# Moving the expert-row gathers into the second graph layer, and reordering the first stage, of a four-block graph and expert network

## The chip, the cores and the metric

The kernel runs on one core of a Trainium2 chip, as one launch. The metric is device time in microseconds (us) from the launch's start to its end. A core has five engines with queues of their own: TensorE (PE, its weight loads are PEld), VectorE (DVE), ScalarE (ACT), GpSimd (POOL) and SyncE (SP). They meet only through semaphores. [...]

## The reference

There are 6250 nodes with 256 features, 100,000 edges sorted by destination, and a type from 0 to 7 on each edge. Four blocks follow each other, each added to x after a layer norm:

```python
x = x + gnn0(layernorm(x))   # per type r: h = xn @ W[r]; edge scores, softmax per destination, weighted sum of h[src]
x = x + ffn0(layernorm(x))   # argmax of 32 experts: relu(relu(xn @ W1[e] + b1[e]) @ W2[e] + b2[e])
x = x + gnn1(layernorm(x))   # below
x = x + ffn1(layernorm(x))   # top 2 of 8 experts, layer norm, gelu, weighted sum
```

The second graph layer forms one product for every node and then needs, for node i, the rows of edge i alone (the first 6250 edges):

```python
xt = (xn @ weight).reshape(-1, 4, 64)
alpha = softmax(leaky_relu(alpha_l[row] + alpha_r[col], 0.01), axis=1)   # over the 4 heads
tmp = einsum('nh,nhd->nd', alpha[:n], xt[col[:n]])                       # the same for each head
```

## The kernel before, in words

The nodes lie in 49 tiles (NT) of 128 rows (P), the last with 106 rows. `k.x` holds all of x in on-chip memory and stays there through most of the kernel. Every `Stage` has its own buffers and semaphores; its end is a barrier of all engines. Inside a stage each engine has its own program, in the order written, so a wait in it holds all that stands behind it.

**First stage, `relation_rows`.** Loads x, the weights W of the eight types and the attention vectors, and makes for every tile the rows `h_tab` that the edges will gather: `norm.transpose` of the normalised tile, then `product`, eight products of 128 x 264 (L643) and one of 128 x 64 (L648) on PE; ACT copies each to `hb`; SP stores. DVE normalises two tiles ahead (`norm.normalise`, L228) and copies the 64 columns (`half`, L543). Ahead of this loop stand, one after another on DVE: the edge rows (L485), `positions` (L492 to L494), the sums of the first quarter of x (`stats`, L201), the cuts (L504 to L510), the block lines (L513 to L517), the groups (L522 to L533, which end with `at_ok` and let GpSimd gather the edge groups, L365 and L367), the other sums, and the variance and its root for all tiles (`norm.statistics`). Two small products of PE (L628, L630) stand in this chain. On SP the sixteen loads of attention vectors (L411) come after a wait for the first edges (L406), and PE begins only with all of W and all the vectors there (L610). In the tile loop DVE does four pieces of edge work (`turn0` to `turn3`) at tiles 4, 6, 8 and 10 and one (`turn5`) at 30; PE transposes the edge arrays from tile 13 (`TURN0`). GpSimd makes the masks of the windows when `node_tab` has been stored after tile 11.

**`attend0`** sums over the edges of the first layer, with 880 gathers on GpSimd. **`settle`** adds the old x.

**`moe0`** normalises, routes, scatters the rows to their experts, computes them and writes `ys0`. Then (`gather` L1273, `address` L1360, `add` L1366, `tile_stats` L1370) it gathers the result rows of each tile in four buffers, adds them to `k.x` and takes the tile's sums.

**`attend1`** takes mean and root of all tiles (`norm.statistics`), prepares the weights (L1582, L1587, copies L1524 and L1526), and runs the node transform: normalise on DVE, two transposes and the product 128 x 264 on PE (L1598), two copies on ACT (L265 to PE's operand, L1505 to `g`), two stores on SP into `g_tab` and `l_tab` (L1490, L1491). `g` has two buffers, and ACT's copy waits until both stores from the same buffer have landed. When all tables are stored (`tables`), GpSimd gathers two rows a tile (L1471, L1472) in groups of four tiles with two sets of buffers, and DVE does the softmax, the weighted sum and the sums of the new x (L1540 to L1558).

`route1` and `experts1` follow.

## Time and profile before

| | |
|---|---|
| median of 3 runs | 3263.57 us (3260.66 to 3266.58) |
| the profiled execution | 3259.22 us, of which its span is 3257.2 us |
| busy in the span | PE 67%, DVE 55%, ACT 41%, POOL 49% |
| first stage | to about 470 us |
| `attend0`, `settle`, `moe0` up to its last stored row | about 470 to 2006 us |
| gathers and sums of the expert rows | 2006 to 2080 us |
| `attend1` | 2080 to 2320 us |
| `route1` and `experts1` | 2320 us to the end |

The shares are means over stages with different limits. For a change in one stage what matters is which engine or transfer ends each step of that stage. The times of rows are us from the span's start; what stands in brackets is the idle time before an instruction and what ended it.

### The profile page before, as it was taken

The numbers are of one execution on the slowest core, as the hardware profiler recorded it, in microseconds if no ns is written. First come the engines' busy times: TensorE is split into PE (matmuls) and PEld (weight loads), VectorE is DVE, ScalarE is ACT, GpSimd is POOL, SyncE is SP. The second block draws the span as 40 slices with busy tenths as digits, with TensorE's granted clock in tenths as the row PEclk, the third lists the DMA queues.
The fourth block names the chain that finished last, engine by engine and source line by source line (L and its number), as shares of the span: only waits on it lengthen the run. The fifth ranks groups of instructions, "written<-read, shape, count | busy, mean of one in ns | idle before, by whom it ended". The sixth has DMA issues, their size and how long they took to land. (4 is left out here: it accounts for less than half of the span.)

```text
span 3257.2 us, 51141 instructions
## 1 busy us (share of the span) xinstructions
PE 2189.7 (67%) x13091; PEld 1849.9 (57%) x13092; DVE 1780.9 (55%) x4102; ACT 1332.3 (41%) x2969; POOL 1589.4 (49%) x1585
## 2 busy tenths in 40 slices
PE   2999985777777777777626085350430079999998
PEld 1888874656666556565426074230430069999997
DVE  4111125777777777776675434426663365656564
ACT  0444444655565655555301053130111344444443
POOL 1056217777777777777250534327227223334333
PEclk8999986888888888888755588685555589999999
DMA  6355447777765555556542244222302632222221
GB/s 141 126 208 213 193 172 210 214 209 211 208 194 144 145 145 145 144 144 132 53 123 72 78 158 144 68 74 51 97 31 104 210 77 42 46 48 47 48 47 26
DMA packets 225887, 402.34 MB, mean 124 GB/s; under 512 B 58684, under 2 KB 153543, under 8 KB 219086
## 3 DMA queue, kind: packets, MB, share of 16 engines
q0 software_dynamic: 84864, 206.63, 26.2%
q1 hardware_dynamic: 122002, 187.73, 17.3%
q10 hardware_dynamic: 18892, 6.45, 0.9%
q8 instruction: 57, 0.93, 0.1%
q14 instruction: 72, 0.59, 0.1%
HBM read 247.26 MB, written 155.68 MB: 124 GB/s over the span
## 5 line engine op out<-in xcount | busy, mean ns | idle before, releaser
L720 POOL DMA_INDIRECT sum_ring<-h_tab,gnn_edge_row x880 | 839.4, 954 | 268.0 <-issue 260.7
L981 PE MATMUL sum_bank<-sum_ring,sum_one_hot 128*128 128x264 f32 x1760 | 583.0, 494 | 215.2 <-issue 195.7
L981 PEld LDWEIGHTS sum_bank<-sum_ring,sum_one_hot 128*128 128x128 f32 x1760 | 418.7, 247 | 334.5 <-issue 227.0
L1802 POOL DMA_INDIRECT out_dram<-moe_y,moe_to_node x112 | 185.9, 1659 | 383.9 <-ACT moe_y L1828 353.0
L643 PE MATMUL rows_bank<-rows_w_rows,rows_xnT 128*128 128x264 f32 x1568 | 358.6, 387 | 1.7 <-ACT rows_xnT L265 1.7
L643 PEld LDWEIGHTS rows_bank<-rows_w_rows,rows_xnT 128*128 128x128 f32 x1568 | 295.1, 191 | 50.3 <-ACT rows_xnT L265 2.1
L770 ACT ACTIVATE sum_distance_by_lane<-all_iota,gnn_minus_local 128x128 bf16<-128x128 f32 x880 | 267.3, 386 | 0.1
L836 DVE TENSOR_TENSOR sum_ring<-sum_ring,sum_bank 128x1024 f32<-128x1024 f32 x220 | 265.7, 1209 | 0.5 <-ACT sum_ring L784 0.4
L970 PEld LDWEIGHTS sum_bank<-gnn_dst_half,sum_one_hot_T 128*128 128x128 f32 x1760 | 226.2, 205 | 43.9 <-issue 40.3
L970 PE MATMUL sum_bank<-gnn_dst_half,sum_one_hot_T 128*128 x1760 | 230.9, 289 | 28.7 <-ACT sum_one_hot_T L763 14.3
L1960 PE MATMUL moe_bank<-moe_w_low,moe_hidden_high 128*128 x896 | 244.2, 273 | 0.0
L1960 PE MATMUL moe_bank<-moe_w_high,moe_hidden_high 128*128 x896 | 244.2, 273 | 0.0
L1960 PE MATMUL moe_bank<-moe_w_high,moe_hidden_low 128*128 x896 | 244.2, 273 | 0.0
L470 ACT ACTIVATE rows_h_rows<-rows_bank 128x264 f32<-128x264 f32 x392 | 152.9, 390 | 198.5 <-PE rows_bank L643 198.5
L843 DVE TENSOR_TENSOR nodes_acc<-sum_bank,nodes_acc 128x264 f32 x440 | 188.2, 428 | 47.7 <-PE sum_bank L981 19.3
L1844 ACT ACTIVATE moe_hidden<-moe_bank,moe_b_T 128x256 f32<-128x256 f32 x456 | 186.3, 475 | 42.8 <-PE moe_bank L1950 25.5
L543 DVE COPY gnn_dst_half<-rows_bank 128x64 f32<-128x64 f32 x49 | 11.0, 225 | 332.1 <-PE rows_bank L648 332.1
L775 ACT ACTIVATE sum_one_hot<-sum_distance_by_lane,all_ones 128x1024 f32<-128x1024 bf16 x110 | 126.3, 1148 | 147.4 <-PE sum_bank L981 145.5
L1950 PE MATMUL moe_bank<-moe_x_high,moe_w_high 128*128 128x256 f16 x912 | 175.3, 274 | 1.7 <-DVE moe_x_low L1894 1.7
L1950 PE MATMUL moe_bank<-moe_x_low,moe_w_high 128*128 128x256 f16 x912 | 175.3, 274 | 0.0
L1950 PE MATMUL moe_bank<-moe_x_high,moe_w_low 128*128 128x256 f16 x912 | 175.1, 274 | 0.0
L826 DVE TENSOR_TENSOR sum_score<-sum_dst_part,sum_ring 128x64 f32<-128x64 f32 x110 | 24.9, 226 | 266.6 <-DMA sum_ring<-h_tab,gnn_edge_row 266.0
(406 smaller groups left out, 4151.3 us busy)
## 6 DMA issues: line engine op xcount, KB each, us to landing
h_tab<-rows_h_rows SPq DMA_DIRECT2D x49, 1056.0 KB, 3.9
sum_local_rows<-local_tab SPq DMA_DIRECT2D x110, 256.0 KB, 3.8
sorted<-sum_blank_row SPq DMA_DIRECT2D x49, 387.0 KB
moe_stage<-in_L_ffn_W_dram SPq DMA_DIRECT2D x16, 1024.0 KB
moe_tile<-sorted POOLq DMA_DIRECT2D x58, 258.0 KB, 4.1
sum_ring<-h_tab,gnn_edge_row POOLq DMA_INDIRECT x880
sorted<-sum_zero SPq DMA_DIRECT2D x49, 256.0 KB
mask_tab<-rows_masks POOLq DMA_DIRECT2D x7, 1560.0 KB, 7.9
```

Source lines behind the costliest of these rows:

```text
L470: nc.scalar.activation(hb[:, t % 2, r, :], bank[2 + r % 4][:, 0:W0], ACT.Copy).then_inc(h_ok.sem, 1)
L643: last = nc.tensor.matmul(bank[2 + r % 4][:, 0:W0], norm.xT[:, u, c * P:(c + 1) * P], wx[:, c, r, :], start=(c == 0), stop=(c == DC - 1))
L720: nc.gpsimd.indirect_dma_start(ring[:, t % (RING * ST), :], None, k.h_tab, bass.IndirectOffsetOnAxis(k.edge_row[:, t:t + 1], 0)).then_inc( ...
L770: last = nc.scalar.activation(off[:, u * P:(u + 1) * P], k.iota[:, :], ACT.Abs, bias=k.minus_local[:, m * ST + u:m * ST + u + 1])
L836: nc.vector.tensor_tensor(to, to, by, ALU.mult).then_inc(msg_ok, 1)
L843: nc.vector.tensor_tensor(col(k.acc, b), sum_b[g % SG][:, 0:W0], col(k.acc, b), ALU.add).then_inc(added, 1)
L970: last = nc.tensor.matmul(pick_b[n % 2][:, u * R * H0:(u + 1) * R * H0], hotT[:, n % 2, u, :], col(k.dst_half, b[u // G]), start=True, sto ...
L981: last = nc.tensor.matmul(sum_b[j][:, 0:W0], hot[:, m % 2, t, :], ring[:, m % RING * ST + t, :], start=(u == 0), stop=(u == G - 1))
L1802: nc.gpsimd.indirect_dma_start(a["out"], bass.IndirectOffsetOnAxis(to_node[:, n % 2, h:h + 1], 0), y[:, n % 2, h, :], None, bounds_check=N ...
L1844: last = nc.scalar.activation(hg[:, q, m * B1:(m + 1) * B1], bank[q][:, m * B1:(m + 1) * B1], ACT.Gelu, scale=1.0 / (XS * WS), bias=col(b1 ...
L1950: last = nc.tensor.matmul(bank[q][:, m * B1:(m + 1) * B1], w1[pw][:, c, bass.ds(e * F1 + (2 * q + m) * P, P)], xh[px][:, u, c, :], start=( ...
L1960: last = nc.tensor.matmul(bank[6 + u][:, h * D:(h + 1) * D], hh[ph][:, u, m, h * P:(h + 1) * P], w2[pw][:, m, bass.ds(e * D, D)], start=(m ...
```

## The change

Two parts, in two places.

**The expert rows.** `moe0` no longer gathers them; it ends when `ys0` is written. The row numbers are kept as integers in `k.rows0` (one copy of 128 x 49), and the scatters use them directly, without a copy for each tile. `attend1` gathers the rows into eight buffers (`SLOTS`), adds them, takes the sums and makes the node transform in seven chunks of seven tiles (`CH`). On DVE the adds and sums of the next chunk stand between the normalisations of this one; at each chunk's end stand the variance (7 small linked instructions) and, after two adds, the inverse root (5 linked ones), with the square root on ACT between. `g` has eight buffers instead of two, the gathered table rows four sets instead of two, and these gathers take their row numbers from `k.dst_i` and `k.src_i` directly. The sums of the previous group (`tile_stats(n - 1)`) stand in `attend` between the exponents' input and the wait for them. All loops of the stage are written out.

**The first stage.** The attention vectors are loaded first, on SP and ACT side by side; W comes in two halves with a semaphore each; x comes in parts of 6, 12, 15 and 16 tiles, the first on ACT and the others on SP. DVE takes sums, variance and root of the first part alone before the tile loop. All else moves into the loop, at the tiles given in `stats_at` and `turns_at`, and so do the two small products of PE (after tiles 4 and 6). The first edges come in as rows and are turned by PE (two transposes after tile 27).

```diff
-        NF, TURN0 = E // P, 13
+        NF, TURN0 = E // P, 18
...
+        quarter = [0, 6, 18, 33, NT]
...
+            def load_x(j):
+                t0, t1 = quarter[j], min(quarter[j + 1], NT - 1)
+                sp.dma_start(k.x[:, t0:t1, :], a["x"][t0 * P:t1 * P, :].rearrange("(t p) f -> p t f", p=P)).then_inc(loaded[j], 16)
+            vectors(sp, 0, "L0_gnn_attn_src")
+            for j in range(2):
+                sp.dma_start(wn[:, j * R // 2:(j + 1) * R // 2], a["L0_gnn_W"][j * R // 2:(j + 1) * R // 2].rearrange("r (c p) f -> p r c f", p=P)).then_inc(weights[j], 16)
...
+                load_x(1)
                 sp.dma_start(k.first_s.rearrange("(t o) -> t o", o=1), a["dst"][0:NF * P].rearrange("(t p) -> t p", p=P)[:, 0:1]).then_inc(first_st, 16)
...
                     sp.dma_start(rows(k.h_tab.rearrange("(n r) o -> n (r o)", r=R), t * P, P), flat(hb[:, t % 2, :, :])).then_inc(stored.sems[t % 2], 16)
-                    if t == 11:
+                    if t == 1:
+                        sp.wait_ge(rows_ok, 1)
+                        sp.dma_start(k.row_s[0:E].rearrange("(p e) -> p e", p=EP), e_row[:, :]).then_inc(line_st, 16)
+                    if t == 8:
+                        sp.wait_ge(at_ok, 1)
+                        sp.dma_start(k.block_tab.rearrange("(c p) -> p c", p=P), blk[:, :]).then_inc(block_st, 16)
+                    if t == 10:
+                        sp.wait_ge(block_st, 16)
+                        sp.dma_start(blk_row[:, :], line(k.block_tab)).then_inc(block_in, 16)
+                    if t == 4:
+                        sp.wait_ge(pos_ok, 1)
+                        for j, name in enumerate(("dst", "src")):
+                            sp.dma_start(ends_n[:, j, :], a[name][0:NPAD].rearrange("(t p) -> t p", p=P)).then_inc(first_nodes, 16)
...
 
         @block.scalar
...
+            vectors(act, 1, "L0_gnn_attn_dst")
+            act.dma_start(k.x[:, 0:quarter[1], :], a["x"][0:quarter[1] * P, :].rearrange("(t p) f -> p t f", p=P)).then_inc(loaded[0], 16)
...
+            root(0)
+            norm.t_ok.start(act)
...
+                if t in (3, 10, 16):
+                    root((3, 10, 16).index(t) + 1)
...
+            turns_at = {1: edge_rows, 2: positions, 3: cuts, 5: block_lines, 7: groups, 9: turn0, 11: turn1, 13: turn2, 15: turn3, 26: first_edges, 28: keep_first, 32: turn5}
+            stats_at = {0: (stats, 1), 1: (variance, 1), 3: (scales, 1), 6: (stats, 2), 8: (variance, 2), 10: (scales, 2),
+                        12: (stats, 3), 14: (variance, 3), 16: (scales, 3)}
...
+                if t in stats_at:
+                    stage, j = stats_at[t]
+                    stage(j)
...
+                if t == 4:
+                    pe.wait_ge(need_ok, 1)
+                    nc.tensor.matmul(bank[7][0:NT, 0:1], k.before[0:NT, 0:NT], need[:, :], start=True, stop=True).then_inc(start_ps, 1)
+                if t == 6:
+                    pe.wait_ge(diag_ok, 1)
+                    nc.tensor.matmul(bank[7][:, 8:8 + 3 * NT], k.ones[0:NT, :], diag[:, :, :].rearrange("p j b -> p (j b)"), start=True, stop=True).then_inc(lines_ps, 1)
+                if t == 27:
+                    pe.wait_ge(first_ok, 1)
+                    pe.wait_ge(turn_free, 3 * G)
+                    for j in range(2):
+                        last = nc.tensor.transpose(bank[7][:, j * P:j * P + NT], ends_nf[:, j, :], k.ident[0:NT, 0:NT])
+                    last.then_inc(first_ps, 1)
                 if TURN0 <= t < TURN0 + 3 * G:
                     n, j = divmod(t - TURN0, G)
```

```diff
-                pool.sem_inc(begun, 1)
-                nc.gpsimd.indirect_dma_start(k.xs0, bass.IndirectOffsetOnAxis(ids[0:m, u:u + 1], 0), xi[0:m, u, :], None).then_inc(scattered[u], 16)
-            rounds(pool, NT, 4, scatter)
...
-                t = i * 4 + u
-                m = P if not isinstance(t, int) or t < NT - 1 else TAIL
-                pool.wait_ge(row_ok, NT + t + 1)
-                pool.sem_inc(begun, 1)
-                nc.gpsimd.indirect_dma_start(y[0:m, u, :], None, k.ys0, bass.IndirectOffsetOnAxis(ids[0:m, u:u + 1], 0)).then_inc(gathered[u], 16)
-            rounds(pool, NT, 4, gather)
 
         @block.sync
...
-        g = s.sb("rows_out", [P, 2, W])
-        ids = s.sb("rows", [P, 2, 2, 4], I32)
-        got, left = s.sb("gathered", [P, 2, 4, W]), s.sb("row_half", [P, 2, 4, H1])
+        g = s.sb("rows_out", [P, SLOTS, W])
+        got, left = s.sb("gathered", [P, SETS, 4, W]), s.sb("row_half", [P, SETS, 4, H1])
...
+            for t in range(NT):
+                m = P if t < NT - 1 else TAIL
+                if t >= SLOTS:
+                    pool.wait_ge(node_ok, t - SLOTS + 1)
+                nc.gpsimd.indirect_dma_start(y[0:m, t % SLOTS, :], None, k.ys0, bass.IndirectOffsetOnAxis(k.rows0[0:m, t:t + 1], 0)).then_inc(brought[t % SLOTS], 16)
             pool.wait_ge(tables, 1)
...
+            for n in range(GROUPS + 1):
+                if n >= SETS:
+                    pool.wait_ge(used, n - SETS + 1)
+                for u in range(size(n)):
+                    t = n * 4 + u
+                    nc.gpsimd.indirect_dma_start(got[:, n % SETS, u, :], None, k.g_tab, bass.IndirectOffsetOnAxis(k.dst_i[:, t:t + 1], 0)).then_inc(arrived[n % SETS], 16)
+                    nc.gpsimd.indirect_dma_start(left[:, n % SETS, u, :], None, k.l_tab, bass.IndirectOffsetOnAxis(k.src_i[:, t:t + 1], 0)).then_inc(arrived[n % SETS], 16)
...
+            for t in range(NT):
+                sp.wait_ge(g_ok, t + 1)
+                sp.dma_start(k.g_tab[t * P:(t + 1) * P, :], g[:, t % SLOTS, :]).then_inc(stored[t % SLOTS], 16)
+                sp.dma_start(k.l_tab[t * P:(t + 1) * P, :], g[:, t % SLOTS, D + H1:W]).then_inc(stored[t % SLOTS], 16)
...
+            for c in range(CHUNKS):
+                root(c)
+                keep(c * CH)
+                for t in range(c * CH, (c + 1) * CH):
+                    if t + 1 < (c + 1) * CH:
+                        keep(t + 1)
+                    emit(t)
```

The main loop of DVE in `attend1`, and its end:

```diff
+            for c in range(CHUNKS):
+                more = c + 1 < CHUNKS
+                t0, t1 = c * CH, (c + 1) * CH
+                if more:
+                    add(t1)
+                    add(t1 + 1)
+                scales(c)
+                for j in range(CH):
+                    normalise(t0 + j)
+                    if more:
+                        if j + 2 < CH:
+                            add(t1 + j + 2)
+                        stats(t1 + j)
+                if more:
+                    variance(c + 1)
...
+            for n in range(GROUPS + 1):
+                attend(n)
+            tile_stats(GROUPS)
```

## Rows read from the trace of the kernel before

**Rows 1.** Page, costliest groups: the edge gathers on GpSimd.

```profile
L720 POOL DMA_INDIRECT sum_ring<-h_tab,gnn_edge_row x880 | 839.4, 954 | 268.0 <-issue 260.7
```

**Rows 2.** Timeline of the first 83 us: start us, us, engine, line, operation.

```profile
23.71 4.12 SPq L411 DMA_DIRECT2D rows_attn_blocks<-in_L_gnn_attn_src_dram  x8
...
39.30 6.07 PE L616 MATMUL rows_bank<-all_ident,rows_w_natural 128*128 128x128 f32 x32 [39.30 <-DMA rows_attn_blocks<-in_L_gnn_attn_dst_dram]
...
45.21 8.36 PE L623 MATMUL rows_bank<-rows_attn_blocks,rows_w_natural 128*128 128x16 f32 x64
...
54.20 1.28 ACT L222 ACT_TABLE_LOAD   x1
...
79.01 0.74 DVE L228 TENSOR_SCALAR rows_xn<-nodes_acc,rows_mean,rows_rstd 128x256 f32<-128x256 f32 x2 [0.25 <-DVE rows_rstd L286]
...
82.30 8.79 PE L643 MATMUL rows_bank<-rows_w_rows,rows_xnT 128*128 128x264 f32 x32 [1.70 <-ACT rows_xnT L265]
```

**Rows 3.** DMA issues of 0 to 90 us: count, KB each, median us to landing.

```profile
rows_w_natural<-in_L_gnn_W_dram SPq DMA_DIRECT2D x1, 2048.0 KB, 19.3
...
rows_group_rows<-row_line,rows_edge_of_group POOLq DMA_INDIRECT x4, 8.5
```

**Rows 4.** Timeline, two neighbouring tiles late in the first stage.

```profile
442.43 0.23 DVE L543 COPY gnn_dst_half<-rows_bank 128x64 f32<-128x64 f32 x1 [7.19 <-PE rows_bank L648]
...
450.17 0.22 DVE L543 COPY gnn_dst_half<-rows_bank 128x64 f32<-128x64 f32 x1 [7.19 <-PE rows_bank L648]
```

**Rows 5.** Timeline of the first stage: edge tables on VectorE, gathers and masks on GpSimd.

```profile
56.39 0.31 DVE L522 COPY rows_block_lines<-rows_bank 128x147 f32<-128x147 f32 x1
...
61.97 0.99 POOL L365 DMA_INDIRECT rows_group_rows<-row_line,rows_edge_of_group  x1 [16.70 <-DVEq L534]
...
122.61 1.13 DVE L548 TENSOR_SCALAR rows_valid<-rows_lane,rows_of_group 128x256 f32<-128x256 f32 x4
...
353.30 0.84 POOL L391 DMA_DIRECT2D mask_tab<-rows_masks  x1 [0.30 <-POOL rows_masks L389]
```

**Rows 6.** Timeline from the first expert-row gather to the second graph layer.

```profile
2006.54 1.02 POOL L1273 DMA_INDIRECT moe_y<-results,moe_rows  x1 [10.65 <-SPq L1293]
...
2009.56 0.42 DVE L1366 TENSOR_TENSOR nodes_acc<-nodes_acc,moe_y 128x256 f32 x1 [6.67 <-DMA moe_y<-results,moe_rows]
...
2013.63 1.40 DVE L1370 BATCH_NORM_STATS2 nodes_stats<-nodes_acc  x4
...
2077.33 0.43 DVE L1370 BATCH_NORM_STATS2 nodes_stats<-nodes_acc 128x6 f32<-128x256 f32 x1
...
2080.05 0.24 DVE L271 TENSOR_TENSOR gnn_tmp<-nodes_stats 128x49 f32<-128x49 f32 x1 [2.29 <-PEq L116]
```

**Rows 7.** Timeline of the node transform, its start and end.

```profile
2088.35 0.69 DVE L1524 COPY gnn_wT<-gnn_bank 128x512 f32<-128x512 f32 x1 [4.76 <-PE gnn_bank L1582]
...
2093.20 2.12 PE L1598 MATMUL gnn_bank<-gnn_w,gnn_xnT 128*128 128x264 f32 x4
...
2096.69 1.06 PE L1598 MATMUL gnn_bank<-gnn_w,gnn_xnT 128*128 128x264 f32 x4
...
2097.80 1.06 PE L1598 MATMUL gnn_bank<-gnn_w,gnn_xnT 128*128 128x264 f32 x4
...
2171.85 0.39 ACT L1505 ACTIVATE gnn_rows_out<-gnn_bank 128x264 f32<-128x264 f32 x1 [1.25 <-DMA l_tab<-gnn_rows_out]
...
2175.99 0.98 POOL L1471 DMA_INDIRECT gnn_gathered<-g_tab,gnn_rows  x1 [95.87 <-issue]
```

**Rows 8.** Waits of 2092 to 2172 us: total us, times, longest.

```profile
ACT gnn_rows_out L1505 <- DMA l_tab<-gnn_rows_out: 38.8, 44, 1.7
```

**Rows 9.** Windows at its end: busy of PE, PEld, DVE, ACT, POOL; PEclk, DMA share, GB/s.

```profile
2172.00:2174.00 2.00, 0.00 (x0) 0.00 (x0) 0.00 (x0) 1.52 (x2) 0.00 (x0) 1.00 0.30 75
2174.00:2176.00 2.00, 0.00 (x0) 0.00 (x0) 0.00 (x0) 0.00 (x0) 0.01 (x1) 0.53 0.00 0
```

**Rows 10.** Groups by line on GpSimd, 2176 to 2310 us.

```profile
L1471 POOL DMA_INDIRECT gnn_gathered<-g_tab,gnn_rows x49 | 55.6, 1134 | 110.5 <-issue 110.5
```

More of the change, by code:

```diff
@@ L344, in relation_rows, with vectors @@
         block = s.block()
+        def vectors(eng, j, name):
+            eng.wait_ge(cleared, 1)
+            with nc.allow_non_contiguous_dma(reason="attention vectors, one word a lane"):
+                for h in range(H0):
+                    p0 = h * HD0 % P
+                    eng.dma_start(ablk[p0:p0 + HD0, h * HD0 // P, j * H0 + h:j * H0 + h + 1],
+                                  a[name][h:h + 1, :].rearrange("a b -> b a")).then_inc(attn_in, 16)
         @block.gpsimd
@@ L456, in _, with root @@
                 nc.scalar.activation(wd[:, c, :].rearrange("p (r h) -> p r h", r=R), got_v[:, c, :, 1, :], ACT.Copy).then_inc(v_ok, 1)
-            norm.root(act)
+            def root(j):
+                part = slice(quarter[j], quarter[j + 1])
+                act.wait_ge(norm.var_ok, j + 1)
+                nc.scalar.activation(norm.sd[:, part], norm.var[:, part], ACT.Sqrt).then_inc(norm.sd_ok, 1)
+            root(0)
+            norm.t_ok.start(act)
             h_ok.start(act)
-            with nc.allow_non_contiguous_dma(reason="the first edges, one word a node"):
-                for t, name in ((k.dst_i, "dst"), (k.src_i, "src")):
-                    act.dma_start(t[:, :], a[name][0:NPAD].rearrange("(t p) -> p t", p=P)).then_inc(first_nodes, 16)
             norm.keep(act, 0, 0, d_ps)
             for t in range(NT):
+                if t in (3, 10, 16):
+                    root((3, 10, 16).index(t) + 1)
                 if t + 1 < NT:
@@ L533, in _, with variance @@
-            ch.link(nc.vector.tensor_copy(at_i[:, :], got[:, 1, :]))
-            v.sem_inc(at_ok, 1)
-            for j in range(1, 4):
-                stats(j)
-            norm.statistics(v, ch)
+                for t in range(quarter[j], quarter[j + 1]):
+                    last = nc.vector.bn_stats(k.stats[:, t, :], k.x[:, t, :])
+                ch.link(last)
+            def variance(j):
+                part = slice(quarter[j], quarter[j + 1])
+                moments(nc, ch, *(k.stats[:, part, i] for i in (1, 2, 4, 5)), norm.mean[:, part], norm.var[:, part], norm.tmp[:, part])
+                v.sem_inc(norm.var_ok, 1)
@@ L539, in _ @@
+            norm.xn_ok.start(v)
             d_ok.start(v)
@@ L1497, in _ @@
         def _(act):
-            norm.root(act)
-            g_ok.start(act)
-            def emit(i, u):
-                xt_ps.done(act, i * 2 + u)
-                stored.slot(act, i, u)
-                nc.scalar.activation(g[:, u, :], bank[2 + u][:, 0:W], ACT.Copy).then_inc(g_ok.sem, 1)
-            norm.keep(act, 0, 0, xt_ps)
-            with act.Fori(0, (NT - 1) // 2) as i:
-                for u in range(2):
-                    norm.keep(act, i * 2 + u + 1, 1 - u, xt_ps)
-                    emit(i, u)
@@ new lines, in add, with stats, variance @@
+            def add(t):
+                v.wait_ge(brought[t % SLOTS], 16 * (t // SLOTS + 1))
+                m = P if t < NT - 1 else TAIL
+                nc.vector.tensor_tensor(k.x[0:m, t, :], k.x[0:m, t, :], y[0:m, t % SLOTS, :], ALU.add).then_inc(node_ok, 1)
+            def stats(t):
+                v.wait_ge(node_ok, t + 1)
+                nc.vector.bn_stats(k.stats[:, t, :], k.x[:, t, :]).then_inc(stat_ok, 1)
+            def variance(c):
+                part = slice(c * CH, (c + 1) * CH)
+                v.wait_ge(stat_ok, (c + 1) * CH)
+                moments(nc, ch, *(k.stats[:, part, i] for i in (1, 2, 4, 5)), mean[:, part], var[:, part], tmp[:, part])
+                v.sem_inc(var_ok, 1)
@@ new lines, in scales, with normalise @@
+            def scales(c):
+                part = slice(c * CH, (c + 1) * CH)
+                v.wait_ge(sd_ok, c + 1)
+                rsqrt_newton(nc, ch, rstd[:, part], tmp[:, part], var[:, part], sd[:, part])
+            def normalise(t):
+                if t >= 2:
+                    v.wait_ge(t_ps, t - 1)
+                nc.vector.tensor_scalar(xn[:, t % 2, :], k.x[:, t, :], mean[:, t:t + 1], rstd[:, t:t + 1], ALU.subtract, ALU.mult).then_inc(xn_ok, 1)
+            add(0)
+            for t in range(1, CH):
+                add(t)
+                stats(t - 1)
@@ L1523, in _ @@
+            stats(CH - 1)
+            variance(0)
             v.wait_ge(wt_ps, 1)
```

328 lines of the change are left out of this document (149 added, 179 removed).

## Prediction

> **What bounds the kernel now.** I read the page first: no engine is busy over 67% of the span, so stages have to be read one by one. In the sum over edges GpSimd issues 880 gathers, and busy plus idle give (839.4 + 268.0) / 880 = 1.26 us for each [rows 1]. That is GpSimd's pitch; the stage runs at it, whatever PE does, and the change leaves it alone. Then I read the timeline where the change acts.
>
> In the first stage PE does nothing until 39.30 us, prepares weights until about 53.6, and starts the first tile's product only at 82.30 [rows 2]. DVE is the one that is late: its serial chain of edge work, all sums, and root ends with the first normalisation at 79.01, and ACT's issue of two slow DMAs stands in the 3.29 us after it. From there a tile takes 450.17 - 442.43 = 7.74 us, and DVE waits 7.19 of them for PE [rows 4]. So the loop is bound by PE, and its 49 tiles slide as a whole with their start. In it DVE has over 7 us free in each tile.
>
> From 2006.54 to 2077.33 + 0.43 the expert rows come in, one in each 1.26 us; DVE waits for them, and PE is idle [rows 6]. Only then come the root and the node transform: first product at 2093.20, first gather from its tables at 2175.99 [rows 7]. In it PE could take a tile in 2097.80 - 2096.69 = 1.11 us, but ACT waits 38.8 us for stores from its two buffers [rows 8], so a tile takes about 1.6 us ((2171.85 - 2093.20) / 49). The last part, 98 gathers, belongs to GpSimd again.
>
> **The first stage, part by part.** What has to be there before the first product is now: W, x of six tiles, the vectors. The vectors need 8 issues on each of two queues, at 4.12 / 8 = 0.52 us each [rows 2], so W is issued near 5.5 us. W of 2 MB took 19.3 us to land, behind 6 MB of x [rows 3]; now about 2.8 MB have to come before or with it. I bound its landing by 16 and 25 us after the start (the full 19.3 after 5.5 is the upper bound) and take 19, nearer to the lower end, since most of x has moved behind it. The first half is turned meanwhile, so half of 6.07 us remains: 22. The 64 thin products take 8.36 us: 30.5. ACT's copies and root and five small instructions on DVE make 1.8 (an estimate, some 0.2 each [rows 6]), the table load 1.28, and from normalisation to product 1.7 (3.29 in the rows, less ACT's DMA issues): 35.3 [rows 2]. The granted clock might fall during the thin products, which would add up to 3 us; I take 36.5. Gain: 82.30 - 36.5 = 45.8, between 40 and 50.
>
> What moved into the loop must fit. DVE runs two tiles ahead, so an insert may last about 7 us (a tile less one normalisation) before PE waits. The sums of x take 16 x 0.35 = 5.6 us at most (0.35 from four in 1.40 us [rows 6]); the longest arithmetic piece, the groups, took 61.97 - 56.39 = 5.6 us plus 0.7 for four small ones [rows 5]. Both fit, just. Waits are the danger. `turn0` at tile 9 waits for gathers that depend on `groups` at tile 7. By the sum above, `half(7)` is at 36.5 + 9.4 + 7 x 7.74 = 100.1 (9.4: the first tile, 8.79 and the thin product); `groups` ends at 106.3; eight gathers at 1.26 and 8.5 us of landing [rows 1, 3] end at 124.9; with its own 1.8 us (four of 1.13 in all, and a copy [rows 5]) and a normalisation, DVE is ready at 127.1. PE wants that tile at the end of product 10, 123.1. So PE stands about 4 us; with stores of the loop beside these gathers I take 5, between 0 and 15, since nothing shows these gathers under that load. Cuts (tile 3) wait for row numbers that are stored two tiles earlier, which fits by about a tile. Two small products and two transposes on PE cost 1.2 us together. SP's new waits at tiles 1, 4, 8 and 10 stand behind a store with nothing urgent after them; node numbers leave SP after tile 16 instead of 11, but at nearly the same time (16 x 7.74 + 36.5 against 11 x 7.74 + 82.3), so GpSimd's masks still end near 353, far from the stage's end [rows 5]. If that cover went, the stage would end with the masks.
>
> Sum of the first part: 45.8 - 5 - 1.2 = 39.6, range 24 to 50.
>
> **The expert rows and the node transform.** The scatters lose a DVE copy per tile but run at GpSimd's 1.26: nothing. The stage now ends with the last stored result, near 2006.2; a barrier took 2080.05 - 2077.76 = 2.3 us, so the new stage starts near T = 2008.5 and its last sum of 2077.8 no longer counts [rows 6]. From T:
> - First sum after 0.3 + 3.0 (2009.56 - 2006.54), six more at 1.26, an add, a sum: T + 11.7 [rows 1, 6].
> - Variance, seven small linked instructions. The same on 49 columns takes 0.24 each [rows 6]; for 7 columns I take 0.19: T + 13.0. The copies of the weights took until 2.8 us after 2088.35 [rows 7]: T + 15.9. Two adds and five small ones: T + 17.6.
> - A full chunk: DVE needs 1.08 us a tile (an add, a sum, a normalisation, 0.35 to 0.37 each in a run), PE 1.11 [rows 7]: 7.8. At the seam stand the last sum 0.35, variance 1.3, two adds 0.75, scales 0.95; with hand-overs 3.4. So 11.2 us, six times, is 67.2. GpSimd needs 7 x 1.26 = 8.8 for the same tiles and has eight buffers, so it stays ahead.
> - The last chunk 7.8, then turn, product and copy 2.6: T + 95.2. From ACT's last copy (2171.85 + 0.39) to the first gather took 3.75 [rows 7]: T + 99 = 2107.5, against 2175.99. The eight store buffers end the waits of 38.8 us [rows 8], but SP still needs two issues per tile, about 1.05 us at the pitch of rows 2, just under PE's pitch.
>
> Gain 68.5. Bounds: if DVE's instructions don't overlap at all (1.24 us a tile, links at 0.24) a chunk is about 13 and the gain 55; if the gathers set the pace (48 x 1.26 + 3.3, then a last chunk and tail of 17) it is 86.
>
> The 98 table gathers never waited for their two sets: idle before them is issue [rows 10]. Four sets and row numbers without a copy therefore give nothing. Their mean of 1134 ns against 954 comes in stretches where DVE works on long operands, and that stays [rows 1, 10]. In the final group four sums of 1.40 us now stand before the wait for the exponents instead of in idle time: 1.1 us lost. Second part: 67.4, range 50 to 85.
>
> **Sum.** 3259.22 - 39.6 - 67.4 = 3152.2. The median of the runs lies 4.35 above the profiled execution: 3156.
>
> **A rule of the Trainium skill against this.** After the node transform, with PE idle, the granted clock is still 1.00 (2.4 GHz) from 2172 to 2174, and 0.53 on average in the next two microseconds, so it falls to 0.50 (1.2 GHz) [rows 9]. At the low level four products took 2.12 us, at the high 1.06 [rows 7]. The Trainium skill, "TensorE: Matmul & The Clock Gate", "HAM oscillation — how this bites in real kernels", says that pauses between bursts of matmuls can bring the clock down again each time. Here each seam of chunks makes such a pause; by that rule the time would be that of the first rival.
>
> **The rivals.**
> - *The clock falls at every seam.* For it: rows 9, and a pause of PE that I estimate at 2 to 2.5 us (the seam less PE's last tile). Against: in those rows it is still up in the first stretch after PE's last work. Price: two tiles per chunk at 2.7 instead of 1.11, about 3 us, less a little caught up, times seven: 19. Time 3175. Chance 0.15.
> - *Waits in the first loop hold PE again and again.* For it: five inserts wait for a DMA or PE, and W took 19.3 us to land once [rows 3]. Against: most have a tile or more of slack. Four more stalls of a tile: 31 us; time 3187. Chance 0.15.
> - *The gathers, not DVE, set the chunks' pace* (if adds and sums overlap better and seams are cheaper): 3156 - 17 = 3139. Chance 0.1.
> - *The new stage doesn't overlap:* sums first, then the transform, because gathers run late under a busy DVE. Only the first part and the store waits remain, about 60: 3204. Chance 0.03.
> - *Slower:* PE runs the first loop at the low clock, as it would if DVE's inserts broke up its work. Eight times 2.12 instead of 1.06 is 8.5 us a tile; from 13 of the 49 tiles on (107 / 8.5) the change loses, at 20 tiles the time is 3156 + 170 = 3326. Against: before, the loop ran beside masks and four turns without one pause. Chance 0.02.
>
> **How the numbers follow.** The forecast has 0.55, range 3138 to 3174. The range for 8 in 10 takes in the first and third rival and most of the second: 3130 to 3190. About 0.2% (6.5 us) is what a measurement of this kernel can tell from no change; slower by more has 0.02, within it 0.01, faster 0.97.
>
> **What would show it.** First stage: the first L643-like product near 36 us; the first loop's end near 425 instead of 465; PE's only pause near 123 us, before the transpose of tile 12; a later start of W would show in PE's first row. Second: the stage begins near 2008 less the first gain; chunks of 11 us on DVE, with PE idle at their seams alone; ACT's waits for stores gone; granted clock 1.00 through the chunks; the first table gather 99 us after the stage's start; 133 us for the gathers as before. The prediction would be wrong if a chunk took over 14 us, if PE paused in several tiles of the first loop, or if the table gathers changed their pitch.

## The result, and the profile after

The changed kernel takes 3162.49 us (median of 4 runs, 3159.72 to 3165.93), where the kernel before takes 3265.07 (3260.66 to 3267.99): ratio 0.9685, with a 95% interval of 0.967 to 0.970. Forecast were 3156, with 3138 to 3174 as its range and 3130 to 3190 as the range for 8 in 10. The profiled execution took 3159.72 us, 7.5 more than the sum of 3152.2.

The gain is 99.1 us of span (3257.2 to 3158.1). The seams of the stages divide it (a load here is a group of four tiles, taken at its first issue; all in us):

| stretch | forecast | measured |
|---|---|---|
| start to the first scatter to the experts (1809.95, now 1773.98) | -39.6 | -36.0 |
| scatters of the rows to the experts' order (68.5, now 68.3) | 0 | -0.3 |
| first to last load of the experts' tiles (114.9, now 122.7) | 0 | +7.9 |
| last load to the first table gather (182.65, now 115.35) | -68.5 | -67.3 |
| from there to the end (1081.2, now 1077.8) | +1.1 | -3.4 |

The timeline of the first 50 us after, against [rows 2] (in all rows a name with q, as SPq, is the queue or sequencer of that engine):

```profile
12.85 5.13 PE L675 MATMUL rows_bank<-all_ident,rows_w_natural 128*128 128x128 f32 x32 [12.85 <-DMA rows_w_natural<-in_L_gnn_W_dram]
...
17.82 9.39 PE L683 MATMUL rows_bank<-rows_attn_blocks,rows_w_natural 128*128 128x16 f32 x64
...
26.80 8.05 SPq L412 DMA_DIRECT2D nodes_acc<-in_x_dram  x2
...
32.25 5.75 PE L699 MATMUL rows_bank<-rows_w_rows,rows_xnT 128*128 128x264 f32 x16
34.89 4.14 SPq L430 DMA_DIRECT2D nodes_acc<-in_x_dram  x1
39.08 2.49 SPq L432 DMA_DIRECT2D node_tab<-rows_row_zero  x1
41.65 1.24 ACT L495 ACTIVATE rows_h_rows<-rows_bank 128x264 f32<-128x264 f32 x4 [9.03 <-SPq L90]
42.10 5.51 PE L699 MATMUL rows_bank<-rows_w_rows,rows_xnT 128*128 128x264 f32 x16 [4.10 <-ACT rows_h_rows L495]
```

W's first half is there at 12.85, and PE turns both halves without a pause, where all of W was forecast for 19; so the first product starts at 32.25 instead of 36.5. But it stops after four of its eight relations: ACT waits 9.03 us for SP's line 90. That line opens the row buffers (`stored.start(sp)`), and in SP's order it stands behind the issues of x and one small store, which take from 26.80 to 41.57; before them SP stood 6.1 us until the first edges had landed (L426). The first tile ends at 48.04, 15.8 us after its start instead of the 9.4 of the forecast.

The same loop at tiles 8 to 11, against [rows 4, 5]. The four rows of L596 (`half`, L543 before) mark the ends of tiles 8, 9, 10 and 11; the last line is the only wait of PE from 117 to 132 (total us, times, longest):

```profile
110.86 0.22 DVE L596 COPY gnn_dst_half<-rows_bank 128x64 f32<-128x64 f32 x1 [1.03 <-PE rows_bank L704]
...
118.60 0.23 DVE L596 COPY gnn_dst_half<-rows_bank 128x64 f32<-128x64 f32 x1 [5.55 <-PE rows_bank L704]
118.62 3.73 PE L699 MATMUL rows_bank<-rows_w_rows,rows_xnT 128*128 128x264 f32 x16
...
124.53 1.24 ACT L495 ACTIVATE rows_h_rows<-rows_bank 128x264 f32<-128x264 f32 x4 [5.33 <-DMA h_tab<-rows_h_rows]
124.97 5.47 PE L699 MATMUL rows_bank<-rows_w_rows,rows_xnT 128*128 128x264 f32 x16 [2.62 <-ACT rows_h_rows L495]
...
128.71 1.14 DVE L601 TENSOR_SCALAR rows_valid<-rows_lane,rows_of_group 128x256 f32<-128x256 f32 x4 [9.89 <-DMA rows_group_dst<-dst_line,rows_edge_of_group]
...
130.87 0.23 DVE L596 COPY gnn_dst_half<-rows_bank 128x64 f32<-128x64 f32 x1
...
138.95 0.22 DVE L596 COPY gnn_dst_half<-rows_bank 128x64 f32<-128x64 f32 x1 [6.41 <-PE rows_bank L704]
```

```profile
PE rows_bank L699 <- ACT rows_h_rows L495: 2.6, 1, 2.6
```

Three tiles take 138.95 - 110.86 = 28.1 us, where three times 7.74 are 23.2: a stall of the length that was forecast, 4.9 us. PE waits 2.62 of them, and then four relations take 5.47 us instead of 3.73, at a lower clock (0.84 on average from 118 to 129). Two waits stand there: DVE's for the edge groups, as forecast, and ACT's for a stored row, which was not. And the one that holds PE in this kernel is ACT's, in the middle of tile 10's product. By the time PE comes to the transposes of tile 12, DVE's wait is just over (128.71, normalised at 130.9). Had ACT not held it, PE would have come there near 126.1 and waited 4.8 us for DVE (an estimate: one tile earlier 7.5 us lie between the product's start at 110.88 and the next transposes at 118.40).

A seam of chunks in the second graph layer, where [rows 7] had one loop (the last row is the first gather from the tables):

```profile
2005.42 0.17 DVE L274 TENSOR_TENSOR gnn_tmp<-gnn_tmp 128x7 f32<-128x7 f32 x1
...
2007.98 0.39 ACT L1541 ACTIVATE gnn_rows_out<-gnn_bank 128x264 f32<-128x264 f32 x1 [0.50 <-PE gnn_bank L1666]
2008.27 0.20 ACT L1529 ACTIVATE gnn_sd<-gnn_var 128x7 f32<-128x7 f32 x1
...
2008.50 0.20 DVE L282 RECIPROCAL gnn_rstd<-gnn_sd 128x7 f32<-128x7 f32 x1 [1.39 <-ACT gnn_sd L1529]
...
2010.06 0.44 PE L1658 MATMUL gnn_bank<-all_ident,gnn_xn 128*128 128x128 f32 x2 [2.11 <-DVE gnn_xn L1580]
...
2080.32 0.98 POOL L1503 DMA_INDIRECT gnn_gathered<-g_tab,nodes_dst_i  x1 [29.64 <-SPq L1522]
```

The variance is there at 2006.2, but ACT takes the root only behind its last two copies (DVE waits 1.39 us for it), and PE stands 2.11 us. The reciprocals, one for each chunk, start at 1995.62, 2008.50, 2019.38, 2032.14, 2042.97, 2055.47 and 2066.31: three chunks of 10.8 to 10.9 us, and three of 12.5 to 12.9. The windows say why (busy time of PE, PEld, DVE, ACT and POOL, then the granted clock, DMA share, GB/s):

```profile
1996.00:2002.00 6.00, 4.45 (x13) 3.36 (x14) 5.53 (x19) 1.54 (x4) 4.60 (x5) 0.50 0.35 106
2002.00:2023.00 21.00, 15.47 (x79) 12.03 (x79) 16.40 (x60) 9.28 (x28) 13.79 (x15) 0.99 0.85 176
2023.00:2027.00 4.00, 4.00 (x15) 3.08 (x14) 3.19 (x11) 1.44 (x4) 3.12 (x3) 0.61 0.57 150
2027.00:2047.00 20.00, 14.78 (x76) 11.58 (x75) 16.06 (x60) 8.73 (x27) 11.61 (x12) 0.99 0.82 163
2047.00:2050.00 3.00, 3.00 (x10) 2.36 (x9) 2.54 (x9) 1.43 (x4) 2.39 (x3) 0.50 0.62 132
2050.00:2073.00 23.00, 18.15 (x93) 14.29 (x93) 14.94 (x55) 10.54 (x32) 0.68 (x1) 1.00 0.37 101
```

The clock is low in three of seven chunks, the long ones: the first from its start, behind a long idle stretch, and the other two only after PE has resumed work behind a seam. At 2021.15 PE's transposes still take 0.44 us and at 2022.13 too, and only the four products from 2022.41 on take 1.65 and then 1.97 us instead of 1.06. The pause before these two chunks was 2.33 and 2.06 us, those before the chunks of 10.8 to 10.9 us 2.07 to 2.11.

### The profile page after: what moved, and what is told of

Read it like the earlier page. It is cut to its first block and busy times, and to the rows that moved or that the text cites. A ratio compares the mean times of both kernels' runs of the same rounds, so it can differ in the third digit from the quotient of the medians.

```text
span 3158.1 us, 49641 instructions
## 1 busy us (share of the span) xinstructions
PE 2201.9 (70%) x13093; PEld 1863.9 (59%) x13094; DVE 1782.5 (56%) x4090; ACT 1326.0 (42%) x2973; POOL 1590.8 (50%) x1585
## 5 line engine op out<-in xcount | busy, mean ns | idle before, releaser
L596 DVE COPY gnn_dst_half<-rows_bank 128x64 f32<-128x64 f32 x49 | 11.0, 225 | 295.6 <-PE rows_bank L704 295.6
```

## The experiments

Two halves first. Both are the changed kernel with functions of the kernel before put back: in the first `moe0` and `attend1`, in the second `relation_rows`.

**The first stage alone.**

> The new first stage alone; the expert rows are gathered and the second graph layer runs as in the kernel before. If the two parts of the change are independent, the first loop's barrier comes 37 us earlier, as in the changed kernel's trace (433.3 instead of 470.6), and all behind it shifts by as much: 3265 - 37 = about 3228 us median. Rival: the middle of the program pays for an earlier start. In the changed kernel the loop over the experts' tiles ran 7.9 us longer (124.8 instead of 116.9) with the granted clock at 0.50 for longer; if the first stage's new timing does that, the loop is 124 to 125 us here too and the median is about 3236. If the 7.9 us belong to the changed second half, the loop is 117 here.

Measured: 3236.06 us (3227.99 to 3242.58), ratio 0.990 (0.987 to 0.993). The first scatter comes at 1775.34, 34.6 us earlier than before (36.0 in the whole), so the stage gives nearly what it gives in the whole. The loop over the experts' tiles took 130.8 us, though this half leaves its code as it was: the rival's 3236 is met, but by a longer loop than its 124 to 125. Which of the moves within the stage gives how much was not run.

**The second half alone.**

> The first stage as before; gathers of the expert rows, sums, statistics and node transform in chunks of seven, eight row buffers. If independent: the stretch from the end of the experts' tiles to the first gather of the tables shrinks by about 65.5 us (168.5 from the seam at 2009.6 to the old first table gather less the 102.0 from the new stage's start), so 3265 - 65 = about 3200 us median, or 3208 if the loop over the experts' tiles is longer here (125 us instead of 117). Rival: the two parts help each other; then this and the first stage alone together fall short of 102 us or go over it by more than 8.

Measured: 3199.15 us (3191.76 to 3205.16), ratio 0.980 (0.977 to 0.983). From the stage's first gather to the first table gather it takes 100.8 us; before 169.5, in the changed kernel 101.2. The experts' loop took 114.6 us. The halves add up to 29.4 + 66.3 = 95.7 us of medians against 102.6 for the whole; the 7 us between are less than the 16 by which the experts' loop differs from profile to profile. That loop's clock, for the kernel before, the changed kernel and the first stage alone, from the loop's first load on:

```profile
1878.00:1890.00 12.00, 8.73 (x37) 7.07 (x37) 0.90 (x4) 3.52 (x11) 5.63 (x11) 0.50 0.31 96
1890.00:1902.00 12.00, 10.94 (x73) 9.40 (x74) 4.97 (x16) 6.99 (x26) 4.02 (x8) 0.97 0.52 168
```

```profile
1842.00:1854.00 12.00, 9.17 (x37) 7.31 (x38) 0.90 (x4) 3.77 (x12) 5.87 (x11) 0.50 0.33 99
1854.00:1866.00 12.00, 12.00 (x42) 9.98 (x42) 3.23 (x10) 4.39 (x14) 2.82 (x6) 0.50 0.40 121
1866.00:1878.00 12.00, 11.63 (x64) 10.15 (x63) 4.45 (x15) 5.36 (x17) 2.15 (x4) 0.73 0.38 120
```

```profile
1844.00:1856.00 12.00, 9.43 (x38) 7.62 (x39) 0.90 (x4) 3.80 (x12) 5.99 (x12) 0.50 0.36 103
1856.00:1868.00 12.00, 10.94 (x75) 9.37 (x74) 4.96 (x16) 6.84 (x24) 3.96 (x8) 0.99 0.53 169
1868.00:1880.00 12.00, 12.00 (x49) 10.00 (x49) 4.34 (x13) 5.52 (x16) 2.89 (x6) 0.58 0.48 153
1880.00:1892.00 12.00, 12.00 (x47) 10.45 (x48) 3.12 (x11) 3.94 (x12) 2.16 (x4) 0.50 0.31 101
```

Once the first loads are through, PE at the low level is busy all the time with 42 to 49 instructions in 12 us, instead of 73 to 75. The clock comes up once and stays (before), comes up late (changed), or comes up, falls under a busy PE and comes up again (first stage alone).

**The row buffers opened early.** In `relation_rows`:

```diff
+            stored.start(sp)
             vectors(sp, 0, "L0_gnn_attn_src")
...
                 sp.dma_start(k.node_tab[0:1, :], ends_f[:, :]).then_inc(node_st, 16)
-                stored.start(sp)
```

> The changed kernel, with the two increments that open the row buffers put ahead of everything else that SP issues. Theory: ACT's fifth copy waited for them, since SP reaches them only after it has issued the loads of x (26.8 to 41.6), and PE stood behind ACT; the first tile took 15.8 us instead of 9.2. Without that wait the first half row is kept near 41.4 instead of 48.0 and the barrier comes 6.6 us earlier: about 3156 us median. Rival: PE waits for something else next (a half of W, x, or tile 9's gathers, whose own chain starts from the loads and not from the loop): then tile 0 is faster but PE stands longer before tile 12 (4.9 us in the changed kernel, up to 11.5 here), and the median stays at 3162.

Measured: 3157.53 us (3150.58 to 3168.57), ratio 0.967 (0.965 to 0.970). The medians' difference from 3162 is within the scatter; the profile isolates the effect:

```profile
31.96 8.56 PE L699 MATMUL rows_bank<-rows_w_rows,rows_xnT 128*128 128x264 f32 x32
...
40.95 0.23 DVE L596 COPY gnn_dst_half<-rows_bank 128x64 f32<-128x64 f32 x1 [9.01 <-PE rows_bank L704]
```

All eight relations run in one piece, the first tile ends 7.1 us earlier, and so does the last (421.00 instead of 428.12). At the first scatter to the experts 3.3 of the 7.1 us are left (1770.73 instead of 1773.98); from the loop's end to there the profiles on chips with fast transfers differ by up to 5 us anyway. The stall at tiles 9 to 11 stays at 4.9 us: the gathers start from the loop's tile 7 and slide with it.

**The turning two tiles later.** In `relation_rows`; the store of the node rows and the reload of their ends move by two tiles as well:

```diff
-7: groups, 9: turn0, 11: turn1, 13: turn2, 15: turn3,
+7: groups, 11: turn0, 13: turn1, 15: turn2, 17: turn3,
-        NF, TURN0 = E // P, 18
+        NF, TURN0 = E // P, 20
```

> The changed kernel, with the four steps that turn the gathered edge groups moved from tiles 9, 11, 13, 15 to 11, 13, 15, 17 and what hangs on them two tiles later. Theory: DVE stood 9.9 us at tile 9 for the gathers of the edge groups, and PE 4.9 us behind it; tile 11 starts DVE's part at about 134, by when the gathers have landed (128.7), so both waits go and the barrier comes 4.9 us earlier: about 3158 us median. Cost: the masks end some 15 us later, near 361, still under the loop that ends at 428. Rival: a later chain (masks or gates) then ends last, and nothing is gained or some us are lost.

Measured: 3164.07 us (3159.80 to 3167.24), ratio 0.968 (0.966 to 0.971). DVE's wait is gone, the stall is not: 112.14 to 140.15 for the same three tiles, 28.0 us.

```profile
119.90 12.86 SPq L436 DMA_DIRECT2D h_tab<-rows_h_rows  x2
...
126.34 1.24 ACT L495 ACTIVATE rows_h_rows<-rows_bank 128x264 f32<-128x264 f32 x4 [5.86 <-DMA h_tab<-rows_h_rows]
126.78 5.20 PE L699 MATMUL rows_bank<-rows_w_rows,rows_xnT 128*128 128x264 f32 x16 [3.16 <-ACT rows_h_rows L495]
```

The store of tile 8 lands late while the edge groups' gathers run, ACT has no free buffer for tile 10, and PE waits 3.16 us for ACT. So my reading of the stall by DVE's wait alone fell. Two kernels separate the two waits:

**Three row buffers, alone and with the later turning.** `hb` gets a third slot and the stores a third semaphore; `turned` lies over `wn`.

```diff
-        stored = Landed(s, "h_rows_stored", 2)
+        stored = Landed(s, "h_rows_stored", 3)
-        hb = s.sb("h_rows", [P, 2, R, W0])
+        hb = s.sb("h_rows", [P, 3, R, W0])
```

> The changed kernel with three buffers of stored rows in the first stage instead of two (the third takes the place of the turned edge groups, which are laid over the weights' natural copy, no longer read by then). The changed kernel's tile 10 ends 12.3 us after tile 9 instead of 7.7: ACT waited 5.3 us there for a store that landed late while the edge groups' gathers ran. At the same place DVE waited 9.9 us for those gathers. Moving DVE's part away alone gave nothing: tile 10 still took 12.5 us. Theory now: each of the two waits alone holds PE by about 4.5 us, so the third buffer alone gives nothing either: tiles 9 to 11 take 20.3 us (15.5 without a stall). Rival: only the late store matters, and DVE's wait is covered: tiles 9 to 11 take 15.5 to 16 us and the first loop ends 4.5 us earlier.

> Both at once: three buffers of stored rows, and the turning of the edge groups two tiles later. Theory: with both waits gone tiles 9 to 11 take 15.5 us and the first loop ends 4.5 to 5 us earlier than in the changed kernel (its last half row at 423.5 for a first one at 48.0). Rival: the gathers slow something else, and some of the 4.5 us stays.

Both ran, once each, on a chip with slower transfers (the kernel before takes 3605 us there), so they are compared with each other within the first loop. The two expectations count from the end of tile 9 to that of tile 11, two tiles (20.3 us, or 15.5 without a stall); here, as above, three are counted, from the end of tile 8. The third buffer alone takes 110.06 to 140.28, 30.2 us; both together 112.50 to 135.72, 23.2 us, which is three tiles without any stall. With the third buffer alone PE no longer waits for ACT, but 4.91 us for DVE:

```profile
128.16 1.14 DVE L601 TENSOR_SCALAR rows_valid<-rows_lane,rows_of_group 128x256 f32<-128x256 f32 x4 [9.19 <-DMA rows_group_dst<-dst_line,rows_edge_of_group]
...
130.41 0.69 PE L236 MATMUL rows_bank<-all_ident,rows_xn 128*128 128x128 f32 x2 [4.91 <-DVE rows_xn L228]
```

Two waits in parallel, and each by itself costs the three tiles 4.8 us or more (4.8 for ACT's, 7.0 for DVE's on the chip with slower transfers): taking away either gives nothing. Of the 4.9 us that go with both, the loop as a whole keeps less. From the first half row to the last it takes 377.0 us where the changed kernel takes 380.1, because with the later turning tiles 33 and 34 take 9.12 and 8.13 us instead of 7.74 each.

**No seams.** In `attend1`: the last sums and the variance of the next chunk move ahead of this chunk's last normalisation, and ACT's root ahead of its copies; PE and ACT lead by a tile across chunks.

```diff
-                        stats(t1 + j)
-                if more:
-                    variance(c + 1)
+                        if j + 2 < CH:
+                            stats(t1 + j)
+                        elif j + 2 == CH:
+                            stats(t1 + j)
+                            stats(t1 + j + 1)
+                            variance(c + 1)
...
+            for t in range(NT):
+                if t % CH == CH - 2 and t + 2 < NT:
+                    root(t // CH + 1)
```

> The changed kernel with the seams between the chunks of seven closed: the next chunk's last statistics and its variance go ahead of the last normalisation but one, ACT takes the root before its last copies instead of behind them, and PE and ACT lead by a tile over the seam. Theory: a chunk takes 7.8 us of work and some 3.4 us of seam, in which PE stands 2.1 to 2.5 us for ACT's root (2008.27) that comes 2.1 us after the variance (2006.2). Without seams the loop of 49 tiles takes about 49 x 1.11 = 54.4 us plus its cold start, so the first gather of the tables comes near T+83 to T+88 instead of T+102: 14 to 19 us less, 3146 us median give or take the experts' loop. The granted clock, which fell to 0.50 at two of the seams, should then stay at 1.0 after the first chunk. Rival: the gathers (1.25 us each) become the pace: 49 of them and 7 before the loop give 61.3 us and the table gathers start no earlier than T+88.

Measured: 3156.23 us (3154.05 to 3161.98), ratio 0.966 (0.964 to 0.969). First gather to first table gather: 90.4 us, 10.8 less than the changed kernel's 101.2, where 14 to 19 were expected. Only 6.3 of them show in the medians; in the profiled execution the experts' loop took 129.9 us instead of 122.7. The clock stays up, but a chunk takes 9.9 us and not 7.8:

```profile
2011.00:2063.00 52.00, 44.37 (x228) 34.46 (x227) 48.27 (x171) 26.46 (x80) 32.78 (x31) 0.99 0.85 180
```

DVE is busy 48.27 of 52 us. With the seam closed its twelve small instructions per chunk (some 2.3 us) no longer stand in a gap, and 7 x 1.08 + 2.3 = 9.9. DVE is the bound there, neither PE (44.37) nor the gathers (32.78).

**One chunk of 49** (`CH = 49`): sums first, then the loop.

> The changed kernel with one chunk of 49 tiles: all sums and statistics first, then one root and the whole loop; the order within the stage is that of the kernel before, in the new stage. This is the change without its overlap. Theory: sums at the pace of the gathers, 3.8 + 48 x 1.25 = T+64, variance, root and scales 2.5, then the loop without seams 49 x 1.11 + 4 = 58: the first gather of the tables at T+126 to T+130, 24 to 28 us later than in the changed kernel, so 3187 us median. Rival: the overlap is worth more, as the forecast's fourth case had it (3204, 45 us more), or nothing, if the seams cost as much as the overlap gives (3162).

Measured: 3201.53 us (3194.66 to 3204.96), ratio 0.979 (0.977 to 0.982), 39 us above the changed kernel. From first gather to first table gather 135.9 us, 34.7 more than in the changed kernel, between the theory's 24 to 28 and the rival's 45. That the median comes out near the rival's 3204 is not all the stage's doing: in the profiled execution (3204.96) the experts' loop took 131.1 us, 8.3 more than in the changed kernel's.

**Two store buffers** instead of eight for `g`.

> The changed kernel with two buffers instead of eight for the rows that are stored to the tables (the sums keep their eight). Theory: a buffer comes free only when its store has landed, some 2.9 to 3.4 us after the copy, so two tiles take that long and the pace is 1.7 us a tile, as in the kernel before (49 tiles in 83 us), instead of 1.11: 49 x 0.6 = 29 us more less what the seams hide (2 us each), so the first gather of the tables at T+115 to T+131 and about 3180 us median. Rival: with the sums between the tiles the stores are hidden: no change, 3162.

Measured: 3200.56 us (3191.74 to 3220.34), ratio 0.981 (0.977 to 0.986); 143.5 us, more than either theory had. The waits of the stage:

```profile
ACT gnn_rows_out L1542 <- DMA l_tab<-gnn_rows_out: 46.7, 27, 4.8
...
DVE gnn_rstd L282 <- ACT gnn_sd L1530: 42.4, 6, 8.5
```

Beside the gathers a store is waited for up to 4.8 us, where the longest wait in [rows 8] was 1.7. And the root of the next chunk stands in ACT's queue behind two copies that wait so: 42.4 us of DVE's time at six seams, where the changed kernel has 8.4. That step was in neither theory, and its 34 us are most of the 42.3 by which the stretch grew. Together with the last experiment: neither overlap nor buffers 169.5 us (the kernel before, which has a barrier in this stretch as well), overlap with two buffers 143.5, eight buffers without overlap 135.9, both 101.2.

**Two sets** of table rows (`SETS = 2`).

> The changed kernel with two sets of four table rows in flight instead of four. Theory: POOL issues the 98 gathers back to back, 1.13 to 1.33 us each, and never waits for DVE in either kernel, so the sets are worth nothing: first to last table gather 130 us as before, 3162 us median. Rival: with two sets POOL waits for DVE (attention of four tiles takes some 10 us): the stretch grows by 2 us or more.

Measured: 3163.97 us (3155.64 to 3169.52), ratio 0.968 (0.966 to 0.971). First to last table gather 130.5 us against 130.1: the sets give nothing.

**Everything at once:** early opening, three row buffers, later turning, no seams.

> All that the runs speak for: the row buffers opened before SP's loads (-7.1 us in the first tile), three row buffers and the turning two tiles later (-4.5), and no seams in the node transform (-14 to -19). Sum: 26 to 31 us under the changed kernel's 3162, about 3133 us median; the experts' loop adds or takes up to 10 by its granted clock. Rival: the gains of the first stage are lost again in the sum over the edges behind it, and only the seams count: 3146.

> The kernel with everything at once, again: on the chip of its first run the kernel before took 3605 us, and every kernel's transfers were slower in the sum over the edges (156 GB/s there instead of 217 in the same stretch), so that run stands beside the others by its ratio alone (0.9659, as much below 1 as the changed kernel's 0.9685). Measured one by one the parts give 7.1 (row buffers opened early), 3 to 5 (third buffer with the later turning) and 10.8 (no seams): where the kernel before takes 3265, about 3141 us median, ratio 0.962. Rival: the 21 us are lost for the most part in the stretches between (a longer low clock in the experts' loop): 3155 or more, ratio 0.966 again.

Measured: 3482.89 us and ratio 0.966 (0.963 to 0.969) on the chip with slow transfers; on the second one 3145.82 us (3138.51 to 3158.95), ratio 0.963 (0.961 to 0.966). Its last half row is copied at 418.79 instead of 428.12, tiles 9 to 11 take 23.2 us, and the seam stretch 89.5. It is the fastest here, some 17 us under the changed kernel. The two stretches give the 21 us that were expected (9.3 and 11.7), and the experts' loop, at 127.1 us, takes 4.3 of them back in the profiled execution.

## Why the prediction was right

The forecast of 3156 stands 6.5 us from 3162.49, but its misses have both signs. Of the span's gain 3.6 us too many were forecast up to the first scatter, 7.6 in a middle that was taken as unchanged and 1.2 up to the first table gather, and 4.5 too few from there to the end. Both gains are there with the causes that were named, except where a line below says otherwise.

- *First product at 36.5:* 32.25. The term for W was too large: the thin products ended at 27.2 instead of 30.5. The rest of the sum held (5.0 us from there to the product, 4.8 forecast), and the thin products took 9.39 instead of 8.36, at a granted clock of 0.75 against 0.85 before: the fall that I had allowed for.
- *The first tile takes 9.4:* 15.8. This step missed a queue: `stored.start(sp)` stands behind SP's issues of x, which were moved past it. I had followed what SP's new waits hold up and not what an increment behind its long issues releases. The first two misses cancel for the most part (-4.3 and +6.4), which is luck, and the early opening shows the second by itself.
- *PE stands 5 us before tile 12:* 4.9 us, but inside tile 10's product, and what held PE in the changed kernel was ACT's wait for a late store (2.62 us, and 1.74 more at the lower clock). DVE's wait, the named cause, is real, and it would have been sufficient, as three row buffers alone show; here it was hidden behind the other. The size came out right because two waits of like length end at one place. That is luck too.
- *Masks hidden:* the last of them go out at 345.33, far ahead of 428. *Elsewhere PE doesn't pause:* from the first product to 430 PE waits for ACT at these two places only (4.1 and 2.6 us). The other tiles take 7.74 us, nine of them 8.1 to 8.3 with small products or transposes of PE in them. So the rival of repeated waits fell. The granted clock is 1.00 on average from 50 to 428, so the slower case fell too.
- *The middle unchanged:* it was 7.6 us longer, the largest miss of the sum. The experts' loop is 114.6 to 131.1 us long in the profiled executions of this study (114.6 for three changed kernels and 114.9 before, 130.8 and more for two others), with the granted clock at 0.50 for longer in the long ones. The half that leaves this loop's code alone had 130.8 and the half that changes `moe0` 114.6, so a long loop does not need the edit to `moe0`. That the new timing of the first stage makes a long loop likelier is not excluded: the two profiled kernels with the old first stage had 114.9 and 114.6, those with the new one 114.6 to 131.1, and the first stage alone gave 29.4 us of median where its first scatter came 34.6 us earlier. What sets the length stays open. It fits the scatter of some 10 to 20 us between runs of one kernel (the kernel before ran in 3259.55 us at a mean clock of 0.804 and in 3278.97 at 0.794), but that this loop makes that scatter was not shown.
- *Chunks of 11.2:* 10.8 to 10.9 at the high clock, 12.5 to 12.9 where it fell. PE's pause at the seam was 2.11 us (2 to 2.5 forecast), 1.39 of it passed on from DVE's wait for the root behind ACT's copies.
- *The clock falls at every seam* (rival): in part. It was low in three of seven chunks, at 1.9 us each instead of 3: 5.6 us instead of 19. The Trainium skill's rule of pauses that bring the clock down ("TensorE: Matmul & The Clock Gate", "HAM oscillation — how this bites in real kernels") is borne out in part. Without the pauses, in the kernel with no seams, the clock stayed at 0.99 from 2011 to 2063; with them it fell behind two of six, and pauses of the same length left it up.
- *T + 99:* 102.0 from the stage's start at 1978.34, so 3.0 too few: three cold chunks are 5.6, less what the other chunks saved. The stage itself starts 13.4 us after the last load, where 2008.5 - 1993.34 = 15.2 were forecast, and so the stretch from last load to first table gather is 1.2 us off (-67.3 against -68.5).
- *Gathers set the pace* (rival): POOL waited 12.4 us for DVE, so it was ahead. *No overlap* (rival): priced at 3204; run as one chunk, 3201.5, with a long experts' loop in it.
- *Four sets and ready row numbers give nothing:* the gathers took 130.1 us from first to last instead of 132.0, and two sets changed nothing; the ready row numbers were not run by themselves. *1.1 us lost in the last group:* from the last table gather to the next scatter 111.0 instead of 110.0. The 2.5 us that the kernel gains behind that scatter were not forecast, and no run explains them.

## What to carry to other kernels

When an issue of a DMA is moved on a queue, list all that stands behind it, increments that open a buffer above all; moving one ahead cost nothing here. When two waits of like length end at the same place, each alone explains the stall and removing either gives nothing, so look for the second before promising a gain. An overlap and the buffers that it needs are worth more together than apart (68 us against 26 and 34): with two buffers the copies that wait for stores stand, in ACT's queue, ahead of the root that the overlapped stage needs next.

## What the runs showed of the hardware

- PE's granted clock fell to 0.50 in a stretch in which PE was busy 10.94 of 12 us before and 12.00 of 12 in it (experts' loop, first stage alone). That loop took from 114.6 to 131.1 us in the profiles of kernels that have the same code in it, the longer the more of it ran at 0.50.
- Stores landed later beside indirect gathers here; that the gathers are the cause was not isolated. For the changed kernel, the DMA issues of 109 to 129 us, beside the edge groups' gathers, and of 200 to 400 us (count, KB each, median us to landing); ACT's wait of 5.3 us is this difference:

```profile
h_tab<-rows_h_rows SPq DMA_DIRECT2D x2, 1056.0 KB, 12.3
rows_group_rows<-row_line,rows_edge_of_group POOLq DMA_INDIRECT x4, 10.2
rows_group_dst<-dst_line,rows_edge_of_group POOLq DMA_INDIRECT x4, 10.6
```

```profile
h_tab<-rows_h_rows SPq DMA_DIRECT2D x26, 1056.0 KB, 4.0
```

  The stores of `attend1` in the changed kernel, of 1997 to 2048 us beside the gathers of the expert rows and of 2052 to 2078 behind the last of them. With two store buffers the median beside the gathers was 2.5 us, against 2.3 before:

```profile
g_tab<-gnn_rows_out SPq DMA_DIRECT2D x29, 132.0 KB, 3.8
```

```profile
g_tab<-gnn_rows_out SPq DMA_DIRECT2D x18, 132.0 KB, 2.6
```

- One of the four chips that the experiments ran on took 3605 us for the kernel before, the others 3262 to 3265. Of the last kernel, run on two of them, the 260 us from 440 on, early in the sum over the edges, moved 156 GB/s there and 216 elsewhere, and from its first to its last edge gather that sum took 1414.0 us there and 1106.5 elsewhere.
